# Two graph layers on one core: the first graph's preparation in another order

## The reference

```python
e_k   = leaky(einsum('bid,bjd->bij', h * a_k[:, 0], h))        # k = 0..3, slope 0.2
alpha = sigmoid(where(adj == 1, e0, where(adj == 2, e1, ...)))  # no code: -max, sigmoid 0
x = layernorm(x + einsum('bij,bjd->bid', alpha, h) + bias)

Hh = x @ W;  s = Hh @ a[:D];  d = Hh @ a[D:]
e  = where(adj != 0, exp(-leaky_relu(s[:, None] + d[None, :], 0.2)), 0)
x  = layernorm(x + elu((e @ Hh) / rowsum(e)))
```

## Time and profile before

| what | value |
|---|---|
| median of three runs | 1442.86 us (1442.67 to 1449.2) |
| the profiled execution's own time | 1447.32 us |
| its span in the trace | 1445.6 us |
| busy: PE, DVE, ACT, POOL | 1346.6, 1063.0, 935.2, 854.3 us |
| PE busy, share of the span | 93% |
| bytes by DMA | 68.18 MB, mean 47 GB/s |

### The profile page before, as it was taken

One profiled execution on the slowest core, in us unless ns is written; L12 is line 12 of the kernel. 1 busy time (PEld: TensorE's weight loads), 2 busy tenths in 40 slices (PEclk: granted clock), 3 DMA queues, 4 the chain that ended last, 5 costly groups with the idle time before them and its releaser, 6 DMA issues.

```text
span 1445.6 us, 29637 instructions
## 1 busy us (share of the span) xinstructions
PE 1346.6 (93%) x8898; PEld 1206.4 (83%) x8898; DVE 1063.0 (74%) x2654; ACT 935.2 (65%) x2197; POOL 854.3 (59%) x1228
## 2 busy tenths in 40 slices
PE   4799999999999999999999999999999999999986
PEld 3688888988889888888988889888988888888875
DVE  3487877777777777877777777787877787777754
ACT  3676757667585666757657685676757657575742
POOL 3464847558384664837557394764838557384732
PEclk9799999999999999999999999999999999999988
DMA  4113031221303213131321303222121322303100
GB/s 105 30 30 74 23 50 60 45 64 29 76 18 51 65 30 75 22 50 54 51 58 32 73 18 51 65 37 68 25 47 54 51 62 33 69 18 51 37 1 31
DMA packets 55185, 68.18 MB, mean 47 GB/s; under 512 B 5488, under 2 KB 38640, under 8 KB 55152
## 3 DMA queue, kind: packets, MB, share of 16 engines
q0 software_dynamic: 18432, 33.56, 14.8%
q1 hardware_dynamic: 36720, 34.22, 7.3%
HBM read 84.55 MB, written 16.78 MB: 70 GB/s over the span
## 4 chain that ended last, share of the span: by engine, by line
PE 52%; POOL 20%; DVE 11%; issue 7%; DMA 5%; ACT 3%; DVEq 1%; POOLq 0%; SPq 0%; ACTq 0%
PE acc_bank L1203 17%; POOL coef_lo L346 9%; PE hh_bank L1182 5%; DMA code_nat<-in_adj 4%; PE acc_bank L1089 4%; PE acc_bank L1090 4%; PE acc_bank L1091 4%; PE lg_bank L1089 4%; PE lg_bank L1091 4%; PE lg_bank L1090 4%; DVE coef L865 3%; POOL rstd L367 3%; PE tr_bank L1124 3%; POOL rstd L357 2%; POOL var_eps L354 2%
## 5 line engine op out<-in xcount | busy, mean ns | idle before, releaser
L1203 PE MATMUL acc_bank<-H,coef 128*128 128x258 f32 x2048 | 472.9, 384 | 8.9 <-ACT reluP L589 8.1
L1203 PEld LDWEIGHTS acc_bank<-H,coef 128*128 128x128 f32 x2048 | 383.6, 191 | 64.5 <-issue 10.6
L346 POOL TENSOR_TENSOR coef_lo<-coef,coef_hi 128x1024 fp32r<-128x1024 f32 x128 | 306.0, 2391 | 75.1 <-ACT coef_hi L538 73.4
L1089 PE MATMUL acc_bank<-h_hi,coef_hi 128*128 128x256 f32 x1024 | 300.2, 293 | 0.0
L1090 PE MATMUL acc_bank<-h_lo,coef_hi 128*128 128x256 f32 x1024 | 289.0, 282 | 0.0
L1091 PE MATMUL acc_bank<-h_hi,coef_lo 128*128 128x256 f32 x1024 | 288.6, 282 | 0.0
L865 DVE SCALAR_TENSOR_TENSOR coef<-G,E_col,codeT 128x256 f32<-128x256 f32 x512 | 229.3, 513 | 43.0 <-PE acc_bank L1203 36.8
L1089 PEld LDWEIGHTS acc_bank<-h_hi,coef_hi 128*128 128x128 f32 x1024 | 197.3, 193 | 1.1 <-issue 0.2
L1090 PEld LDWEIGHTS acc_bank<-h_lo,coef_hi 128*128 128x128 f32 x1024 | 197.6, 193 | 0.0
L1091 PEld LDWEIGHTS acc_bank<-h_hi,coef_lo 128*128 128x128 f32 x1024 | 197.3, 193 | 0.0
L332 POOL DMA_DIRECT2D code_nat<-in_adj x128 | 73.5, 575 | 202.1 <-PE tr_bank L1124 181.5
(11 more groups left out here) (80 smaller groups left out, 2613.3 us busy)
## 6 DMA issues: line engine op xcount, KB each, us to landing
code_nat<-in_adj POOLq DMA_DIRECT2D x128, 256.0 KB, 3.6
x_raw<-in_x SPq DMA_DIRECT2D x16, 1024.0 KB, 5.6
out<-x SPq DMA_DIRECT2D x128, 128.0 KB, 1.7
W_ext<-in_L_gnn_W SPq DMA_DIRECT2D x1, 256.0 KB, 2.8
score<-in_L_gnn_a SPq DMA_DIRECT2D x1, 256.0 KB, 6.0
bias_bc<-in_L_gnn_bias SPq DMA_DIRECT2D x1, 128.0 KB, 3.9
a_col<-in_L_gnn_a SPq DMA_DIRECT2D x4, 1.0 KB, 2.1
```

The lines of the kernel that those rows point to most:

```text
L346: nc.gpsimd.tensor_tensor(coef_lo[:, t % 4, :, :], blocks(coef[:, t % 4, :]), f32(coef_hi[:, t % 4, :, :]), ALU.subtract).then_inc(S.lo0, 1)
L1089: nc.tensor.matmul(dst, lhs_hi, rhs_hi, start=first, stop=False)
L1203: ins = nc.tensor.matmul(acc_bank[t % 2][:, 0:HC], coef[:, SLOT1[t], J * P:(J + 1) * P], H[:, J, :], start=J == 0, stop=J == NT - 1)
```

## The change

Nothing is computed differently; the order is another one, and waits are moved.

- SP issues `x_raw` of graph 0 first, then the four `a_col` loads, which have a semaphore of their own (`a_loaded`), then the other three weights.
- POOL issues the first four adjacency loads ahead of everything else. It waits for the weights and x as before, makes `xb`, issues loads 4 and 5, makes `h_lo`, and issues loads 6 and 7.
- `a_bc` gets a tile of its own (before, it lay in a part of `score`), so the first scaling no longer waits for `weights_ready`.
- DVE extends `W_ext` behind the four `low_xT`, not ahead of them.
- ACT waits for `a_loaded` only, does its four `high_x` behind the four `high_xT`, and copies no codes; DVE copies all eight tiles.
- PE, ACT and DVE interleave codes, scores, tanh, mirrors and masks by rows.

The diff, with what is only an indentation left out:

```diff
+        a_bc = sb("a_bc", [P, 2 * D])
...
-        a_bc = score[:, 3, 0:2 * D]
...
+        a_loaded = sem("a_loaded")
...
-        N_WEIGHT_DMAS = KINDS + 3
+        N_WEIGHT_DMAS = 3
...
         def _(sp):
+            sp.dma_start(x_raw[:, :, :], x_v[0, :, :, :]).then_inc(F.x_loaded, 16)
             for k, ak in enumerate((a0, a1, a2, a3)):
...
-                    sp.dma_start(a_col[:, k, :], ak.rearrange("(c p) o -> p (c o)", p=P)).then_inc(weights_loaded, 16)
+                    sp.dma_start(a_col[:, k, :], ak.rearrange("(c p) o -> p (c o)", p=P)).then_inc(a_loaded, 16)
...
-            load_x(F, 0)
...
         def _(pool):
+            for t in range(4):
+                pool.dma_start(code_nat[:, t, :], adj_v[0, t, :, :]).then_inc(F.adj_loaded[t], 16)
...
-            for t in range(4):
-                load_adj(F, 0, t, True)
             for t in range(NT):
                 add_bias(F, 0, t)
+            for t in range(4, 6):
+                load_adj(F, 0, t, False)
             for c in range(4):
                 low_x(F, 0, c)
-            for t in range(4, NT):
+            for t in range(6, NT):
                 load_adj(F, 0, t, False)
...
-                    if isinstance(b, int) and b == 0:
-                        act.wait_ge(weights_ready, 1)
-                    else:
+                    if not (isinstance(b, int) and b == 0):
                         act.wait_ge(F.mask0, NT * b)
...
-            act.wait_ge(weights_loaded, 16 * N_WEIGHT_DMAS)
+            act.wait_ge(a_loaded, 16 * KINDS)
             for c in range(4):
                 high_xT(F, 0, c, False)
+            for c in range(4):
                 high_x(F, 0, c)
-            for J in ROWS:
+            for J in (7, 6, 5, 0, 1):
                 scale_row(0, J)
-            for t in range(NT):
-                keep_codes(F, 0, t, False)
-            for J in range(NT):
+            for J in range(3):
                 tanh_row(0, J)
-            act.wait_ge(consts_made, 4)
+                scale_row(0, J + 2)
+            tanh_row(0, 3)
             for t in range(4):
                 high0(F, 0, t, False)
+                tanh_row(0, t + 4)
+            act.wait_ge(consts_made, 4)
...
+            def extend_weights():
...
-            for c in range(4):
+            for c in range(2):
                 low_xT(F, 0, c, False)
-            for J in ROWS:
+            keep_codes(0, 0)
+            keep_codes(0, 1)
+            for c in range(2, 4):
+                low_xT(F, 0, c, False)
+            extend_weights()
+            for J in (7, 6, 5):
                 leaky_row(0, J)
-            for t in range(4):
+            for J in range(3):
+                keep_codes(0, 2 * J + 2)
+                keep_codes(0, 2 * J + 3)
+                leaky_row(0, J)
+            for t in range(2):
+                mask0_below(0, t, False)
+                mask0_rest(0, t)
+                leaky_row(0, t + 3)
+            for t in range(2, 4):
                 mask0_below(0, t, False)
                 mask0_rest(0, t)
...
-            for c in range(4):
-                if c >= 2:
-                    pe.wait_ge(F.xT_lo, c - 1)
-                transpose_x(F, 0, c)
-            pe.wait_ge(F.xT_lo, 4)
-            for J in ROWS:
-                scores(0, J)
-            for t in range(NT):
+            def first_codes(t):
                 if t >= 2:
                     pe.wait_ge(F.codes_kept, t - 1)
                 transpose_codes(F, 0, t)
-            for t in range(4):
+
+            transpose_x(F, 0, 0)
+            transpose_x(F, 0, 1)
+            first_codes(0)
+            first_codes(1)
+            for c in range(2, 4):
+                pe.wait_ge(F.xT_lo, c - 1)
+                transpose_x(F, 0, c)
+            pe.wait_ge(F.xT_lo, 4)
+            for J in (7, 6, 5):
+                scores(0, J)
+            for J in range(3):
+                first_codes(2 * J + 2)
+                first_codes(2 * J + 3)
+                scores(0, J)
+            for t in range(2):
                 mirror(0, t)
+                scores(0, t + 3)
+            mirror(0, 2)
+            mirror(0, 3)
```

More of the change, by code:

```diff
@@ L720, in _ @@
             nc.vector.tensor_copy(H[:, :, D + 1], sd_sq[:, :, 0]).then_inc(setup_step, 1)
[L721 to L734, removed]
+            def extend_weights():
+                dve.wait_ge(weights_loaded, 16 * N_WEIGHT_DMAS)
+                steps = 4
+                for which, col in ((1, D), (0, D + 1)):
+                    for dt in range(KD):
+                        nc.vector.tensor_tensor(reluP[:, 0, :], W_ext[:, dt, 0:D], a_bc[:, which * D:(which + 1) * D],
+                                                ALU.mult).then_inc(setup_step, 1)
+                        dve.wait_ge(setup_step, steps + 1)
+                        ins = nc.vector.tensor_reduce(W_ext[:, dt, col:col + 1], reluP[:, 0, :], AX.X, ALU.add)
+                        steps += 2
+                        if which == 0 and dt == KD - 1:
+                            ins.then_inc(weights_ready, 1)
+                        else:
+                            ins.then_inc(setup_step, 1)
+                            dve.wait_ge(setup_step, steps)
             def low_xT(S, b, c, general):
@@ L771, in keep_codes @@
                 dve.wait_ge(F.codes, NT * b + t + 1)
-                dve.wait_ge(F.codes_kept, NT * b + t)
-                dve.wait_ge(F.mask1, NT * b + t + 1 - NT)
-                dve.wait_ge(F.codes_watched, NT * b + t + 1 - NT)
+                if not (isinstance(b, int) and b == 0 and t == 0):
+                    dve.wait_ge(F.codes_kept, NT * b + t)
+                if not (isinstance(b, int) and b == 0):
+                    dve.wait_ge(F.mask1, NT * b + t + 1 - NT)
+                    dve.wait_ge(F.codes_watched, NT * b + t + 1 - NT)
                 nc.vector.tensor_copy(codeT[:, t, :],
```

## The result

The changed kernel takes 1471.54 us (median of six runs, 1467.42 to 1476.13), the kernel before, run beside it, 1445.34 (1442.67 to 1449.2). The ratio is 1.0182, with a 95% interval of 1.0157 to 1.0206: slower by 26 us, where I had forecast 9 us less. The spans of the profiled executions are 1470.3 and 1445.6, a difference of 24.7 us.

What follows compares the result with a forecast made beforehand. PE waits for one stage after another until the first aggregate at 61.35 us, then the loop goes at PE's pace. Terms -2.0 - 5.7 - 1.4 = -9.1 took 1442.9 to 1433.8 us, range 1429.5 to 1439.

Steps and rivals of the forecast that it cites:

- given back: The loop's first graph waits for something with a time of its own, half the gain is lost, 1438.4 us; chance 0.06.
- Term 1: Loads at the start: x first, adjacency beside it, lets ACT start earlier, -2.0 us.
- early rival: Start: x's load is not held up by POOL's queue, a gain of 6.7 us, time 1429.1; chance 0.13.
- late bound: ACT's start at 12.9 us, with x, adjacency and column loads all served, a gain of 1.3 us.
- Term 2: ACT's start to row 5's scores: extension of W on DVE takes 3.6 us plus 2.0 for meeting POOL, ending at 29.8.
- collide fully: DVE's extension of W meets POOL's pieces, 5.0 us at most, 3.0 more than counted, time 1436.8; chance 0.1.
- Term 3: Interleaved scores, codes and mirrors from 30.1: PE work 20.3 us, waits 0.3, aggregate at 55.6 against 61.35, -5.7.
- Term 4: First aggregate: PE's clock stays at full where it was half before, -1.4 us, or 0 if it falls.
- low-clock rival: PE stays at half clock through the interleaved scores, rows 0 to 4: 13.6 us more, time 1447.4; chance 0.05.

## Why the prediction was wrong

**The step that failed** is the one that reads: "each microsecond there should come through to the end, since nothing in the later part is timed against the start". As for data and semaphores no run speaks against it: with the loop in a good place, the median is 7.2 us lower (1439.42 against 1446.65), and the summing of the first tile moved from 65.78 to 58.05, by 7.7. But I looked for what ties the loop to the start only in time (loads, phases), and the tie is one of place: 15 more instructions on DVE ahead of the loop, 13 returns of 2.54 us, +33.0. The rival "given back" had the right question and the wrong size and mechanism, and it was dismissed with a stretch of the kernel before, in which such a cost can't show. All my rivals were about engine time. That the diff adds eight copies and seven waits to a stream with a hardware loop in it could be counted from the diff; the size could not be read from any row of before, only that 18 packets were fetched in all, and none of them from 225 to 1340 us.

**Term 1, the loads (-2.0, right by another way).** ACT's first eviction moved from 15.46 to 12.96, -2.5. I expected x and the columns to end together at 12.1 to 12.9. x came at 6.8, as the early rival had it; the table load ran at 7.97; but `a_col`, on which ACT waits, landed at 12.9, the late bound. So both bounds I weighed were right, each for another load. "At the same moment" was wrong: the adjacency's four issues run from 1.42 to 3.2 and its first packet came at 5.94, when x's were nearly through. The columns, behind x, met it for nearly their whole length. (They are not the last that SP issues: the other three weights stand behind them.)

Where the two queues met, they shared the engines about packet by packet. From 7 to 11 us 443 packets of `a_col`, of 4 bytes each, passed beside 425 of the adjacency's queue, and `a_col` landed 9.0 us after its issue; it took 4.6 where the adjacency was held back. Of x, with `a0`'s column ahead of it, 333 packets passed beside 334, and it landed after 9.9 us; in the changed kernel x hardly met the adjacency and landed after 5.8.

**Term 2, the extension (collision 2.0, was 4.8).** The first product took 5.28 us instead of 0.43 and the other three 0.43: not two products with a microsecond each, but one that stood from the first `h_lo` piece to the end of the fourth. The bound of 5.0, which is the rival "collide fully", was the right value. The extension thus took 8.5 us (21.25 to 29.74) where I had 5.6. It began 0.9 ahead of my count, so row 5 went on at 29.99 and not at 28.1 (30.1 less the shift of 2.0): 1.9 late.

That the two collide is measured; why they do, no run shows. The product's record starts 0.04 us ahead of `h_lo`'s, and it was the product that waited; one POOL piece would have cost it 1.2 us, and it waited for all four. It did so in five more runs (5.14 to 5.20 us in three, 4.40 and 3.94 where it came in the midst of the row), each time to the end of `h_lo`. `h_lo` itself took 4.96 to 5.00 us in these six runs, and 4.95 in the kernel before. DVE's `hT_lo`, with one operand in a bank, took no longer beside POOL: in the run with x in front and ACT waiting for `a0` alone 0.69 us ahead of `xb` (at 10.36) and 0.68 beside it (at 15.91).

**Term 3, the interleaving (the PE work 20.6 with its waits, was 18.2).** From row 5's start, 29.99, PE had no wait until the last score matmul was done at 48.2:

```profile
30.00:34.30 4.30, 4.30 (x23) 0.50 0.24 82
34.30:48.00 13.70, 13.70 (x99) 0.99 0.24 39
```

(Stretches of PE alone: length; busy us and count; PEclk, DMA share, GB/s.) No code copy and no maximum came late. The clock was full from row 0's second matmul on, where I had taken half of row 0 at half clock. The codes took 4.1 us (1.93 and twice 1.07; 4.5 counted), the mirrors 1.75 (2.0), so the scores 12.4 (13.8), and the 0.3 for small waits was not needed: 2.4 in all. The tail, from the last score to the aggregate, is 4.9 us as counted (48.2 to 53.12; 50.7 to 55.6). So the 1.9 lost to the collision came back here, and that is why the aggregate's 53.6 was met to half a microsecond: two errors of opposite sign.

**Term 4, the clock (-1.4, was +1.0).** I took the clock to stay full, since PE's gap ahead of the aggregate would be shorter than before. It did not:

```profile
50.00:51.00 1.00, 0.66 (x4) 1.00 0.03 8
51.00:52.00 1.00, 0.00 (x0) 0.75 0.00 0
52.00:53.00 1.00, 0.00 (x0) 0.50 0.00 0
...
57.00:58.00 1.00, 1.00 (x7) 0.50 0.09 16
```

The clock fell at about 51.5, 3.3 us after the last score matmul (with four transposes of the mirrors between, at 50.20), where before it was 5.2 (42.1 to 47.3: the 0.64 of 47 to 48 us in the earlier trace rows puts the fall there, not at 47.6), and the aggregate ran wholly at half: 5.4 us to the first sum (58.56 - 53.12), not 4.4 as before (65.78 - 61.35). In four other runs the fall came later: with 128 increments and with `a0` first the aggregate began at full clock and the clock fell at 53.7 and 54.1, and it took 4.5 and 4.35 us; with the adjacency held back, and with x in front and ACT waiting for `a0` alone, it began at full clock and took 4.6. So a half-clock stretch stands in each start looked at, and what varies is when it begins. What sets that, the runs don't settle; I should have carried both levels, 1.00 and 0.50, in the range.

So the start without the loop's trouble was worth 7.2 us where I said 9.1: 8.2 up to the aggregate's start (7.7 forecast), less 1.0 for the clock in it (1.4 more forecast). The low-clock rival (rows 0 to 4 at half) didn't occur: the 512-column matmuls of row 0 stood 0.23 us apart from 34.8 on, as before from 30.35 on, 6.2 us after the first score (24.12); up to 30.04 they had stood 0.43 apart.

## What to carry to other kernels

Ahead of a hardware loop count instructions, not only time. Here 15 more on one engine cost 33.0 us over 13 returns in the changed kernel, and 29.4 in the kernel before. After an edit that adds or removes some, compare the instruction queue's packets on the page (here 83 against 18) and the time of one turn (88.99 us against 86.45), and if they rose, shift that engine's loop by a few dozen cheap instructions: 26 and 32 brought the changed kernel back to 18 packets and 86.40 us.

Don't take a load's time from where it runs alone if another queue's packets will come beside it. Here x landed after 5.8 us, and after 9.9 where it took turns with the adjacency, 333 packets to 334 in 4 us; the four columns, a kilobyte each in 4-byte packets, landed after 9.0 us beside the adjacency and after 4.6 where that was held back.

Keep a DVE product like that of `W_ext` and `a_bc` off the critical path where POOL works through a row of pieces: here it took 5.28 us beside `h_lo` and 0.42 elsewhere.

## What the runs showed of the hardware that I had not expected

- A loop of 283 instructions on DVE costs 86.4 us for a turn, or 89.0, by where it begins in the stream; a shift by 128 instructions changes nothing, one by 15 or 26 decides. In the bad place each turn fetches five packets of 8.2 KB, three of them around the return in the turn looked at, and DVE stands for 2.3 us more there; PE then ran for some 3 us at a granted clock of 0.50, and a turn takes 2.5 us more. The branch back takes 2.74 to 3.08 us instead of 0.29 to 0.37.
- The adjacency loads, issued by POOL from 1.42 us on, had their first packet at 5.94, x, issued by SP at 0.88, at 2.02. x landed after 5.8 us; issued at 1.39 behind one small column, after 9.9. Where the two queues met, about as many packets of each passed: 333 of 1.0 KB to 334 of 1.9 KB, and 443 of 4 bytes to 425 of 1.8 KB.
- DVE's product of `W_ext` and `a_bc`, where it met POOL's row of four `h_lo` instructions, ended only behind the row, in each of six runs: it took 5.14 to 5.28 us in four, 4.40 and 3.94 in two, and 0.42 elsewhere.
- The wait that a trace names can be over: PE's last matmul started at 320.49, and DVE, free at 321.4, began at 324.42 "for" it.
